# Last stage of a two-layer transformer kernel: another order of its chunks and preparation, sequences written out, first-layer products in halves

## What is computed

```python
def _L1_ffn_ref(x, router_w, router_b, w1, b1, w2, b2, sw1, sb1, sw2, sb2):
    probs = softmax(xf @ router_w + router_b)            # 64 experts
    tw, ti = top_k(probs, 8); tw = tw / sum(tw)
    # every routed expert: 64 hidden features, its output weighted with its share, 0 if not picked
    routed = sum_e cw[e][:, None] * (silu(xf @ w1[e] + b1[e]) @ w2[e] + b2[e])
    # two shared experts: 512 hidden features each, not weighted
    shared = sum_s silu(xf @ sw1[s] + sb1[s]) @ sw2[s] + sb2[s]
    return routed + shared
x = x + _L1_ffn_ref(_layernorm(x), ...)
```

## Time and profile before

| | us |
|---|---|
| median of the three timed runs | 3076.99 |
| lowest and highest | 3068.58, 3077.08 |
| the profiled execution, its own time | 3072.48 |
| its span, first to last instruction | 3070.8 |

### The profile page before, as it was taken

One profiled execution on the slowest core, in us unless ns is written; L12 is line 12 of the kernel. 1 busy time (PEld: TensorE's weight loads), 2 busy tenths in 40 slices (PEclk: granted clock), 3 DMA queues, 4 the chain that ended last, 5 costly groups with the idle time before them and its releaser, 6 DMA issues. The chain is left out here.

```text
span 3070.8 us, 51829 instructions
## 1 busy us (share of the span) xinstructions
PE 2511.0 (82%) x18511; PEld 2185.4 (71%) x18511; DVE 1789.3 (58%) x3147; ACT 1333.6 (43%) x2052; POOL 810.7 (26%) x1143
## 2 busy tenths in 40 slices
PE   1988888885049999954677777858999999999999
PEld 1766666775049999953555666747888888888888
DVE  5555555545138888857877777626654444544543
ACT  0444444442027767743333333323444444444444
POOL 3444444401520000024565654530000000000000
PEclk9899999986569999987798989988999999999999
DMA  2000000004247777755544444414332222222221
GB/s 83 1 2 1 2 1 1 1 1 140 73 161 235 232 235 237 231 189 131 146 122 124 133 122 120 124 51 144 112 100 84 73 94 79 78 94 80 85 78 59
DMA packets 191329, 311.65 MB, mean 101 GB/s; under 512 B 28308, under 2 KB 100184, under 8 KB 191192
## 3 DMA queue, kind: packets, MB, share of 16 engines
q1 hardware_dynamic: 179112, 272.01, 29.1%
q0 software_dynamic: 12080, 37.76, 3.7%
HBM read 269.84 MB, written 39.85 MB: 101 GB/s over the span
## 5 line engine op out<-in xcount | busy, mean ns | idle before, releaser
L2143 DVE TENSOR_TENSOR e_h_lo<-e_h,e_h_hi 128x512 fp32r<-128x512 f32 x320 | 221.5, 692 | 476.7 <-ACT e_h_hi L2209 475.9
L2196 ACT ACTIVATE e_h<-e_h_ps,e_b 128x512 f32<-128x512 f32 x320 | 220.1, 688 | 486.2 <-PE e_h_ps L2260 455.4
L2274 PE MATMUL e_y_ps<-e_w_hi,e_h_hi 128*128 128x256 f32 x1280 | 365.1, 285 | 24.0 <-DVE e_h_lo L2143 23.9
L2274 PE MATMUL e_y_ps<-e_w_hi,e_h_lo 128*128 128x256 f32 x1280 | 358.0, 280 | 0.0
L2274 PE MATMUL e_y_ps<-e_w_lo,e_h_hi 128*128 128x256 f32 x1280 | 357.3, 279 | 0.0
L2274 PEld LDWEIGHTS e_y_ps<-e_w_hi,e_h_hi 128*128 128x128 f32 x1280 | 239.9, 187 | 56.3 <-DVE e_h_lo L2143 41.6
L2260 PE MATMUL e_h_ps<-e_yT_hi,e_w_hi 128*128 128x512 f32 x640 | 256.4, 401 | 2.5 <-DVE e_yT_lo L2129 2.5
L2260 PE MATMUL e_h_ps<-e_yT_hi,e_w_lo 128*128 128x512 f32 x640 | 253.7, 396 | 0.0
L2260 PE MATMUL e_h_ps<-e_yT_lo,e_w_hi 128*128 128x512 f32 x640 | 253.4, 396 | 0.0
L402 DVE TENSOR_REDUCE a_top<-a_ring 128x2 f32<-128x1024 f32 (+3 forms) x256 | 202.5, 818 | 86.9 <-PE a_ring L603 85.8
L2274 PEld LDWEIGHTS e_y_ps<-e_w_lo,e_h_hi 128*128 128x128 f32 x1280 | 240.2, 188 | 11.7
(11 more groups left out here) (362 smaller groups left out, 6894.5 us busy)
## 6 DMA issues: line engine op xcount, KB each, us to landing
e_w<-in_w SPq DMA_DIRECT2D x78, 1024.0 KB, 5.5
e_spread<-share_store SPq DMA_DIRECT2D x512, 128.0 KB, 2.8
a_keys<-rows_store SPq DMA_DIRECT2D x128, 256.0 KB, 5.1
a_queries<-rows_store SPq DMA_DIRECT2D x86, 256.0 KB, 4.5
a_running_hidden<-rows_store SPq DMA_DIRECT2D x42, 256.0 KB, 4.4
sorted_x<-zeros POOLq DMA_DIRECT2D x10, 1024.0 KB, 16.9
e_xs<-sorted_x SPq DMA_DIRECT2D x39, 256.0 KB, 4.9
sorted_y<-e_ys POOLq DMA_DIRECT2D x39, 256.0 KB, 5.5
```

The source lines that it names most:

```text
L2143: dve.tensor_tensor(h_parts[c % 2][1][:, :], h[:, c % 2, :], h_parts[c % 2][0][:, :], ALU.subtract).then_inc(h_lo.sem, h_lo.tick())
L2196: act.activation(h[:, c % 2, :], h_ps[c % 2][:, :], ACT.Silu, bias=b1[:, c:c + 1]).then_inc(h_ready.sem, h_ready.tick())
L2274: last = pe.matmul(y_ps[n][:, 0:D], h_parts[c % 2][a][:, n * P:(n + 1) * P], w2[b][:, c, :], start=False, stop=(c == CH - 1 and m == 2))
```

## The change

Only `experts1_phase` changes, in five respects.

1. **Shared chunks first.** `ORDER` puts chunks 32 to 39 at positions q = 0 to 7 and the routed ones at 8 to 39. The weights' pieces are loaded in that order. The bias matmuls, which need the shares, move from `down` of position 0 to that of position 8 (`SHARED`); so the shares of a sequence are turned and spread during its own first chunks, not the sequence before.
2. **Preparation in smaller pieces, at other positions.** On DVE: statistics at 10 and 11 (two token blocks each), aggregation at 12, seed at 13, normalising at 18 and 20, logits 28, best eight 29 and 30, exponent 31, matching 32 and 33, keeping 35, shares 36. On PE the transposes follow 22 and 24, logits 26, and the turn of the shares position 0 (3 in the first sequence). ACT's exponential follows 33, in the first sequence 0.
3. **The seam between sequences.** `up` of the next sequence's positions 0 and 1 is issued after `down` of 38 and 39, where it came after the end. The split of the next tokens comes before position 39's end on ACT and DVE, and `silu(39)` behind `high(38)`. The adds into `y_ps` wait for each token block apart.
4. **The start.** SP issues the first two weight pieces ahead of the five small loads; only what reads those waits for them. `up(0)` no longer stands behind the first shares. The weights are split after odd positions as before, now the chunks 32 to 39 first.
5. **All sequences written out**, with waits on constants; and `up` **in two halves** of 256 columns, twelve matmuls where there were six.

```diff
+        ORDER = list(range(ROUTED, CH)) + list(range(ROUTED))
...
-        def turns(engine, prepare, body):
-
-
-            prepare(0, None)
-            body(0, True, True)
-            with engine.Fori(0, B - 2) as i:
-                body(i + 1, True, False)
-            body(B - 1, False, False)
 
...
+            load_piece(0)
+            load_piece(1)
...
+            for i in range(B):
+                if i + 1 < B:
+                    sp.wait_ge(turned.sem, turned.at(KC * (i + 1)))
                     load_tokens(i + 1)
...
+                if i == 0:
+                    load_piece(GROUP + 2)
+                    load_piece(GROUP + 3)
+                store_shares(i)
+                for r in range(SPREADS):
+                    spread_shares(r)
+                if i == 0:
+                    load_piece(GROUP + 4)
+                    load_piece(GROUP + 5)
+                else:
+                    sp.wait_ge(stored.sem, stored.at(16 * i))
+                    load_residual(i)
+                for r in range(ROUTED - SPREADS):
+                    sp.wait_ge(scaled.sem, scaled.at(i * ROUTED + r + 1))
+                    spread_shares(r + SPREADS)
+                    if i == 0 and r % 2 and GROUP + 6 + r // 2 < len(PIECES):
+                        load_piece(GROUP + 6 + r // 2)
+                if i == 0:
+                    sp.wait_ge(w_ready.sem, w_ready.at(len(PIECES)))
+                    load_residual(0)
+                sp.wait_ge(added.sem, added.at(TB * (i + 1)))
+                sp.dma_start(out[i:i + 1, :, :].rearrange("o (n p) d -> p (o n) d", p=P),
...
-            STEPS = {5: "stats", 6: "seed", 10: "norm", 18: "top", 22: "keep"}
...
-            def first_preparation(i, _):
-
-                for at in ("stats", "seed", 0, 1, "norm", 2, 3, "top", "keep", "split"):
-                    if at in range(GROUP):
-                        split_piece(at)
-                    else:
-                        prepare(i, at)
-
-            turns(dve, first_preparation, body)
-
...
+            tiles = range(TB)
+            statistics(0, tiles)
+            aggregate()
+            seed()
+            split_piece(0)
+            split_piece(1)
+            normalise(0, tiles)
+            split_piece(2)
+            split_piece(3)
+            low_tokens(0)
+            take_logits(0)
+            top(tiles)
+            exponents()
+            for i in range(B):
+                for q in range(CH):
...
+                    if q == CH - 1 and i + 1 < B:
+                        low_tokens(i + 1)
...
+                    if i == 0 and q == 0:
+                        match(tiles)
+                    if i == 0 and q == 2:
+                        keep(0)
+                        share()
+                    if i == 0 and q in SPLIT_AT:
+                        split_piece(SPLIT_AT[q])
+                    if i + 1 < B:
+                        if q in (10, 11):
+                            statistics(i + 1, tiles[2 * (q - 10):2 * (q - 9)])
+                        if q == 12:
+                            aggregate()
+                        if q == 13:
+                            seed()
+                        if q in (18, 20):
+                            normalise(i + 1, tiles[q - 18:q - 16])
+                        if q == 28:
+                            take_logits(i + 1)
+                        if q in (29, 30):
+                            top(tiles[2 * (q - 29):2 * (q - 28)])
+                        if q == 31:
+                            exponents()
+                        if q in (32, 33):
+                            match(tiles[2 * (q - 32):2 * (q - 31)])
+                        if q == 35:
+                            keep(i + 1)
+                        if q == 36:
+                            share()
+                dve.wait_ge(res_loaded.sem, res_loaded.at(16 * (i + 1)))
+                for n in tiles:
+                    dve.wait_ge(y_done.sem, y_done.at(TB * i + n + 1))
                     dve.tensor_tensor(x_res[:, n, :], x_res[:, n, :], y_ps[n][:, 0:D], ALU.add).then_inc(added.sem,
                             added.tick())
...
-            STEPS = {12: "turn0", 14: "turn1", 20: "exp", ROUTED - 1: "share"}
...
+            for k in range(KC):
+                turn(0, k)
+            high_tokens(0)
+            act.wait_ge(small.sem, small.at(5 * 16))
+            for i in range(B):
+                more = i + 1 < B
+                silu(i, 0)
+                for q in range(CH):
+                    if q < CH - 2:
+                        silu(i, q + 1)
+                    high(i, q)
+                    if q == CH - 2:
+                        silu(i, q + 1)
+                        if more:
+                            high_tokens(i + 1)
+                    if i == 0 and q == 0:
+                        exponential(0)
+                    if q == (5 if i == 0 else 2):
+                        shares_by_expert(i)
+                    if more and q in (23, 25):
+                        turn(i + 1, (q - 23) // 2)
+                    if more and q == 33:
+                        exponential(i + 1)
...
+            def up(i, q):
+                at, c = i * CH + q, ORDER[q]
+                if q == 0:
+                    pe.wait_ge(y_lo.sem, y_lo.at(KC * (i + 1)))
+                if i == 0 and q % 8 == 0:
+                    pe.wait_ge(w_ready.sem, w_ready.at(GROUP * (q // 8) + 2))
+                if at >= 2:
+                    pe.wait_ge(h_ready.sem, h_ready.at(at - 1))
+                for cols in (slice(0, S // 2), slice(S // 2, S)):
+                    ops = [(w1[a][:, k, c * P:(c + 1) * P], yT[b][:, k, cols]) for k in range(KC) for a, b in TERMS]
+                    for m, (l, r) in enumerate(ops):
+                        last = pe.matmul(h_ps[q % 2][:, cols], l, r, start=(m == 0), stop=(m == len(ops) - 1))
+                last.then_inc(up_done.sem, up_done.tick())
...
-                up(0)
-                up(1)
-                for c in range(CH):
-                    if c + 2 < CH:
-                        up(c + 2)
-                    down(c)
-                    if more and c in STEPS:
-                        prepare(i + 1, STEPS[c])
...
+            for i in range(B):
+                more = i + 1 < B
+                for q in range(CH):
+                    if q < CH - 2:
+                        up(i, q + 2)
+                    down(i, q)
+
+                    if q >= CH - 2 and more:
+                        up(i + 1, q - (CH - 2))
+                    if q == (3 if i == 0 else 0):
+                        turn_shares(i)
+                    if more and q in (22, 24):
+                        turn(i + 1, (q - 22) // 2)
+                    if more and q == 26:
+                        find_logits(i + 1)
 
```

431 lines of the change are left out of this document (184 added, 247 removed).

## The result

| | before | after |
|---|---|---|
| median, 11 runs each, us | 3077.08 | 3058.55 |
| lowest and highest, us | 3068.22, 3102.57 | 3050.15, 3069.63 |
| profiled execution: its own time, us | 3072.48 | 3050.35 |
| its span, us | 3070.8 | 3048.6 |
| PE busy, us | 2511.0 | 2509.8 |

The ratio of the runs is 0.9937, with an interval of 0.9917 to 0.9957. The change makes the kernel faster, by 18.5 us. The forecast was 3040.5 us, so the point lay 18 us too low; the range, 3024 to 3066, held the result.

What follows compares the result with a forecast made beforehand. PE was taken to bound a sequence, leaving waits and matmul pitch to win. From 3072.5 us, start -7.2, first sequence -3.3, late sequences -8.7, last -0.2 and halves -12.6 sum to -32.0: 3040.5 us, range 3024 to 3066.

Steps and rivals of the forecast that it cites:

- Start, -10.1: Before the first `up`: it starts when the logits end, 8.95 us earlier, and earlier statistics add 1.2 us.
- +2.0: Start, given back: the first `down` chain sticks out by 0.9 (before 0.2), and the exponential makes `down(1)` wait 1.3 us.
- - 3.3: First sequence: 3.3 us saved, as its loss falls from 13.7 to 10.4 us.
- 12.3 - 2.3 + 3.9: First sequence's loss before: 12.3 us over a late one, minus 2.3 for the clock, plus 3.9 of ordinary waits.
- The +0.9 for the turn of the shares: Start, given back: the first shares' turn moves from idle time into the first sequence, costing 0.9 us.
- Late sequences, -1.45 each: Six late sequences: smaller DVE pieces remove waits, 2.45 of 3.9 us stay; -8.7 us in all.
- Written out: nothing: All sequences: waits on constants drop register instructions, which run beside other work; no gain or loss.
- The seam: Between sequences: waits before `down(38)` 0.15, next `up(0)` 0.7 and `down(0)` 0.89, together 1.74 us.
- The last sequence, put at -0.2: Eighth sequence: 0.2 us shorter, apart from the halves.
- Halves, -12.6: `up` in 256-column matmuls: between +3.2 us (slow pitch) and -28.5 (fast pitch over `up` and `down`), the middle taken.
- Slower by instruction fetch: Rival: written-out sequences fetch instructions late, 4.5 us each for six, 27 in all; 3083 us, chance 0.05.
- The rival with the slow pitch: Rival: matmuls keep the slow pitch, all else as forecast, -16.2 us; 3056.3 us, chance 0.32.

Runs made afterwards that it cites:

- e9: Changed kernel plus high(0) before silu(1) at seams, exponential among shared chunks, and up(0) waiting per token half; 3041.7 us, ratio 0.988 to the kernel before.
- e2: Changed kernel with `up` of 512 columns again, no halves; 3063.3 us, ratio 0.9945 to the kernel before.
- e3: Kernel before with only the six middle sequences written out instead of looped; 3074.8 us, ratio 0.9996.
- e4: Changed kernel with ACT doing high(0) ahead of silu(1) at each seam; 3044.6 us, ratio 0.9878 to the kernel before.
- e5: Kernel before with `up` in halves and the six middle sequences written out; 3072.1 us, ratio 0.9995.
- e1: Kernel before with only `up` in two halves of 256 columns, loop kept; 3084.1 us, ratio 1.0011.

## Why the prediction was right or wrong

**What bounds the kernel.** Right. PE bounds a sequence, and the waits read from the old trace were the ones that went. With all of them gone in e9, PE is busy for 116.5 of a late sequence's 116.8 us.

**Start, -10.1.** Measured 37.4 - 26.8 = 10.6. The tokens, ahead of everything in the queue, landed 4.4 us after their issue, and `up(0)` stood behind the logits alone.

**First sequence, with what is given back: +2.0 + 0.9 - 3.3 = -0.4, with its share of the pace -2.0.** Measured -3.5 (133.8 to 128.9, less the 1.4 of bookkeeping). e2 has 128.2 there, so in this sequence, where DVE sets the pace for long, the halves gained nothing; the order alone gave -4.2, nearly 4 us more than the count (in which 12.3 - 2.3 + 3.9 is 13.9, not 13.7). This sequence varies by itself, though: e3, which changes nothing in it, has 133.1 for 133.8. Of the 4 us, 1.7 were only booked in the wrong sequence. The +0.9 for the turn of the shares is one part: before, the first sequence already held the turn for the second, so it gains none by the change. It has one turn before,

```profile
2187.00 1.03 PE L2244 MATMUL e_pro_ps<-ident_f,e_kept_one 128*66 128x128 f32 x8
...
2916.22 1.03 PE L2244 MATMUL e_pro_ps<-ident_f,e_kept_one 128*66 128x128 f32 x8
```

where 2916.22 is in the seventh sequence and the last has none, and one after, while the last sequence now has one too:

```profile
2101.73 1.03 PE L2270 MATMUL e_pro_ps<-ident_f,e_kept_one 128*66 128x128 f32 x8
...
2935.62 1.03 PE L2270 MATMUL e_pro_ps<-ident_f,e_kept_one 128*66 128x128 f32 x8
```

It takes 0.8 us from start to the next `up`. The other part is the seam's wait before `down(0)`, 0.9: it was counted with the sequence that ends, and stands behind the next sequence's first `up`. Where the other 2 us were saved wasn't tried.

**Late sequences, -1.45 each.** Right in size. From before to e2 a late sequence went from 121.45 to 120.2, -1.2. Alone, the order gives 0.9 and the writing-out 0.36. "Written out: nothing" was wrong as a statement on the loop, but not as a term: what it cost stood inside the waits behind DVE's pieces, which the prediction had counted among its 3.9 and the change removes.

**The seam.** Its longest wait was forecast as 0.61 + 0.28 and read as 0.61 idle before `down(0)`; e4 took 0.85 away with it. The wait before `up(0)` was forecast at 0.7 and costs 0.4, the one before `down(38)` at 0.15 and costs 0.36, each from start to start; the three come to 1.65, where 1.74 was forecast. What failed is where they were booked. The last sequence, put at -0.2 and -1.8 with its pace, became 0.5 us longer (115.3 to 117.3, less 1.4): it holds the last seam's wait before `down(0)` and a turn of the shares, 1.7 us that the sum had in the first sequence, and its pace gained 1.1 where 1.6 was counted.

**Halves, -12.6.** Right that the fast pitch comes and that the halves gain, wrong in size and in what keeps the pitch: this step carries the miss of the sum. "I take the middle" of +3.2 and -28.5 was a choice between ends without a row that decided it (24 matmuls at 117.7 ns against 2.81 us are +0.015 a chunk, so the slow end is nearer +4.8). Measured: after to e2, 5.7 us. PE's timeline of the kernel after, first matmuls of `up` and `down` in turn:

```profile
2380.69 0.28 PE L2285 MATMUL e_h_ps<-e_yT_hi,e_w_hi 128*128 128x256 f32 x1
...
2382.11 0.28 PE L2301 MATMUL e_y_ps<-e_w_hi,e_h_hi 128*128 128x256 f32 x1
...
2383.53 0.28 PE L2285 MATMUL e_h_ps<-e_yT_hi,e_w_hi 128*128 128x256 f32 x1
...
2384.90 0.28 PE L2301 MATMUL e_y_ps<-e_w_hi,e_h_hi 128*128 128x256 f32 x1
...
2386.26 0.28 PE L2285 MATMUL e_h_ps<-e_yT_hi,e_w_hi 128*128 128x256 f32 x1
```

One chunk takes 2.84 us, the next 2.73, then again 2.84. The stream doesn't keep a pitch "until something interrupts it", as I had put it; it changes over at nearly each passage from `down` to `up` (263 of 281 in this stage; on the way from `up` to `down` 4 of 303). Of some 6700 steps inside groups at one of the two pitches, 45 to 47%, by how they are sorted, had a mean near 113.6 ns and the rest 117.8. The mean, 115.9, against 117.7 all slow would be 14 us for all 7680 matmuls; but the first sequence doesn't use it, a passage and the step behind it cost up to 4 ns extra, and the 512s had cost 116.7 per 256 columns, so it is 0.95 us a sequence. The Trainium skill, "TensorE: Matmul & The Clock Gate", Back-to-back issue gap, was weighed as the rule against this step: by its 2.5 ns per matmul the stage would be 4.8 us longer than without halves. The page gives that formula for a matmul by itself, and another figure for a stream, about 131 ns at 512 columns; the traces here, with fp32r operands, have 233.3. At the slow pitch two halves do take 2.3 ns more than one matmul of 512 columns (235.6 against 233.3), at the fast one 6.3 less (227.0). With everything else equal, twelve matmuls of 256 columns cost less than six of 512, in e5 as in e2's comparison.

**Slower by instruction fetch.** The rival had the right symptom and the wrong side. "Issue" waits of 1.4 to 1.9 us a sequence do exist, in e1: they come with the loop and the longer list, and it is writing out that takes them away. They took 3.5 us more than the halves gave there. In the kernel after none is seen in a late sequence. The first has three in its weight loads, at `down` of 0, 16 and 32, where the matmul itself waits for a low part, as it had three before; its line in the view of waits is

```profile
PEld e_y_ps L2301 <- issue: 2.2, 3, 0.9
```

**The sum.** -32.0 forecast, -26.5 measured: start 0.5 and first sequence 1.5 better than forecast, late sequences in all 5 worse (six times 0.6 of pace, 0.2 of the rest), the last 2.3 worse. In the first and the last of these sequences 1.7 is the booking named above, which cancels. The other 12.5 us to the median lie outside the stage: 4.6 since the sum was made against an execution that fast (3072.5 against the 3077.1 of this comparison), and 8.0 since the medians differ by 18.5 us where the stages differ by 26.5. Of these 8, the two traces have 4.4 ahead of the stage (its anchor is at 2051.84 and at 2056.25); the rest is in no trace. Chance is the likely reason, but it isn't shown: median less stage is 2060 to 2062 us for the kernel before and 2061 to 2075 for the twelve others, each time more than for the kernel before in the same set of runs (by 0.3 to 14.6), and no run asks whether an edit of the last stage can cost something outside it. The rival with the slow pitch, 3056.3, came nearest the median, and the median lies in the band of 3050 to 3064 that was given to it; the trace shows it wasn't what happened. So the range held for its width, with a share of luck: the sum of the stage was 5.5 us off, the point 18.

## What to carry to other kernels

In a pipeline written by hand, order the short steps of an engine by what is due next, not by the loop's pattern: one `high` ahead of one `silu` at each seam was worth 7 us, more than all the halves (5.7). A block that one engine can't shorten (here 3.0 us of an exponential and two table loads) costs nothing where the chunk's own chain is shortest, so look for that place first. Before more instructions go into a hardware loop, look at its jump back; and judge a change of one stage by that stage's own length in the trace when the total varies by more than the change is worth.
